# A mixed-precision 3x3 convolution on one core: image planes stored as a block of even rows and a block of odd rows

## The reference

```python
mask = _predictor_mask(x)                      # mean of 8x8 blocks >= 0.05
x_high = jnp.where(mask, x, EPS)
x_low = jnp.where(mask, EPS, x)
y_high = _conv(_quant_act_uint(x_high, act_scale_high, 8), _quant_weight_per_oc(w_high, 8))
y_low = _conv(_quant_act_uint(x_low, act_scale_low, 4), _quant_weight_per_oc(w_low, 4))
return y_high + y_low
```

## Time and profile before

| what | value |
|---|---|
| median of 3 runs | 664.49 us |
| the profiled execution's own time | 662.33 us |
| its span, first to last instruction | 660.5 us |
| busy share PE / DVE / ACT | 96% / 90% / 73% |
| mean granted TensorE clock | 0.996 |
| DMA, mean over the span | 158 GB/s |

### The profile page before, as it was taken

One profiled execution on the slowest core, in us unless ns is written; L12 is line 12 of the kernel. 1 busy time (PEld: TensorE's weight loads), 2 busy tenths in 40 slices (PEclk: granted clock), 3 DMA queues, 4 the chain that ended last, 5 costly groups with the idle time before them and its releaser, 6 DMA issues.

```text
span 660.5 us, 10672 instructions
## 1 busy us (share of the span) xinstructions
PE 635.5 (96%) x3714; PEld 355.9 (54%) x3714; DVE 594.5 (90%) x739; ACT 483.7 (73%) x491; POOL 10.2 (2%) x30
## 2 busy tenths in 40 slices
PE   3779999999999999999999999999999999999996
PEld 1345555555555555555555555555555555555554
DVE  7899999999999999999999999999999999999933
ACT  6768787777777778778777778777877877877442
POOL 3200000000000000000000000000000000000000
PEclk9989999999999999999999999999999999999999
DMA  6245445533435543334543344553343454331122
GB/s 266 97 154 195 162 174 195 194 134 128 182 140 194 194 158 124 163 146 188 194 186 127 132 177 157 194 194 148 122 175 139 194 194 170 124 150 68 72 97 98
DMA packets 14409, 104.07 MB, mean 158 GB/s; under 512 B 1728, under 2 KB 1728, under 8 KB 10432
## 3 DMA queue, kind: packets, MB, share of 16 engines
q1 hardware_dynamic: 14400, 103.95, 41.2%
HBM read 52.56 MB, written 51.38 MB: 157 GB/s over the span
## 4 chain that ended last, share of the span: by engine, by line
PE 95%; ACT 2%; DVE 1%; DMA 1%; issue 0%; DVEq 0%; SPq 0%
PE psum L336 95%; DMA wraw_l<-w_low 1%; ACT rounded_h L450 0%; ACT psum L485 0%; ACT wT_l L467 0%; DVE pooled L619 0%; DVE w_max_l L578 0%; ACT wT_h L467 0%; PE psum L322 0%; DVE ybuf L717 0%; DVEq L63 0%; DVE wq_l L601 0%; DVE wint_l L585 0%; DVE upper L701 0%; DVE wq_l L590 0%
## 5 line engine op out<-in xcount | busy, mean ns | idle before, releaser
L485 ACT ACTIVATE psum<-psum,ratio 128x1344 f32<-128x1344 f32 (+2 forms) x159 | 174.4, 1097 | 131.0 <-PE psum L336 128.3
L336 PE MATMUL psum<-plane_l,wT_l 128*128 128x448 f16 (+1 forms) x1164 | 211.7, 330 | 0.0
L336 PE MATMUL psum<-plane_h,wT_h 128*128 128x448 f16 (+1 forms) x1164 | 209.5, 328 | 0.0
L336 PEld LDWEIGHTS psum<-plane_l,wT_l 128*128 128x128 f16 x1164 | 112.9, 97 | 83.1 <-issue 2.4
L336 PEld LDWEIGHTS psum<-plane_h,wT_h 128*128 128x128 f16 x1164 | 112.0, 96 | 81.3
L717 DVE SCALAR_TENSOR_TENSOR ybuf<-psum,out_scale_h,shared 128x448 f32<-128x448 f32 (+1 forms) x194 | 114.3, 605 | 27.5 <-PE psum L336 20.1
L619 DVE TENSOR_REDUCE pooled<-xbuf 128x49 f32<-128x3136 f32 (+2 forms) x33 | 109.4, 3315 | 0.0
L506 ACT ACTIVATE shared<-psum,bias,out_scale_h 128x448 f32<-128x448 f32 (+1 forms) x128 | 86.2, 674 | 26.4 <-PE psum L336 23.5
L450 ACT ACTIVATE rounded_l<-xbuf,inv_act_l 128x1568 int16<-128x1568 f32 (+1 forms) x64 | 101.7, 1591 | 4.8 <-DMA xbuf<-x 4.8
L450 ACT ACTIVATE rounded_h<-xbuf,inv_act_h 128x1568 int16<-128x1568 f32 (+1 forms) x64 | 101.9, 1594 | 0.0
L336 PE MATMUL psum<-rowsum_l,wT_l 128*128 128x448 f16 (+1 forms) x384 | 86.9, 335 | 2.3 <-ACT wT_l L467 2.3
(11 more groups left out here) (78 smaller groups left out, 340.4 us busy)
## 6 DMA issues: line engine op xcount, KB each, us to landing
xbuf<-x SPq DMA_DIRECT2D x31, 1568.0 KB, 6.5
y<-ybuf SPq DMA_DIRECT2D x32, 896.0 KB, 3.6
y<-ybuf SPq DMA_DIRECT2D x32, 672.0 KB, 3.9
xbuf<-x SPq DMA_DIRECT2D x1, 896.0 KB, 7.9
xbuf<-x SPq DMA_DIRECT2D x1, 672.0 KB, 5.3
wraw_l<-w_low SPq DMA_DIRECT2D x1, 576.0 KB, 4.1
wraw_h<-w_high SPq DMA_DIRECT2D x1, 576.0 KB, 6.2
act_scales<-scales SPq DMA_DIRECT2D x1, 1.0 KB, 1.8
```

The costliest lines, as they stand in the source:

```text
L336: last = nc.tensor.matmul(out, wT[k][:, mat, :], moving(k, p, band, row, dx), start=(k == "l" and j == 0), stop=(j == len(parts) - 1), ski ...
L485: return nc.scalar.activation(banks, banks, ACT.Identity, scale=ratio[:, 0:1])
```

## The change

A plane is kept as two blocks: the padded even rows (0, 2, 4, ...), one after the other with a step of 58 elements, and behind them, at `ODD`, the padded odd rows. Rows d0 and d2 of all pairs then lie in the even block and d1 and d3 in the odd block, each pair one row further. `moving` reads every operand with a row step of `PITCH`. `apply_mask` writes image rows into the two blocks with two instructions in place of one, so `s_plane` counts twice as fast and those who wait on it wait for twice the count. `row_sums` and `differences` work on flat stretches of the two blocks; a stretch of row sums ends with the two border elements that GpSimd wrote before ("closing"). `outer` becomes two separate stretches, `inner` takes the common row step. The borders change their shapes, not their number.

```diff
-    PLANE = (H + 2) * PITCH + 4
+    ODD = (H // 2 + 1) * PITCH + 4
+    PLANE = 2 * ODD
...
             if row == "d1-d2":
-                return rows(inner[k][band][p], 1 + dx, INNER_PITCH, count)
+                return rows(inner[k][band][p][:, :], 1 + dx, PITCH, count)
             if row in ("d0-d2", "d1-d3"):
-                return rows(outer[k][band][p], (row == "d1-d3") * PITCH + 1 + dx, 2 * PITCH, count)
+                return rows(outer[k][band][p][:, int(row == "d1-d3"), :], 1 + dx, PITCH, count)
             if row is None:
-                return rows(rowsum[k][p], t0 * PITCH + 1 + dx, PITCH, count)
-            return rows(plane[k][p], (2 * t0 + row) * PITCH + 1 + dx, 2 * PITCH, count)
+                return rows(rowsum[k][p][:, :], t0 * PITCH + 1 + dx, PITCH, count)
+            return rows(plane[k][p][:, :], row % 2 * ODD + (t0 + row // 2) * PITCH + 1 + dx, PITCH, count)
...
-                nc.vector.tensor_tensor(
-                    rows(plane[k][p], (a0 * POOL + 1) * PITCH + 2, PITCH, (a1 - a0) * POOL
-                         ).rearrange("p (a y) w -> p a y w", y=POOL),
-                    clipped[k][:, elements(q)].rearrange("p (a y w) -> p a y w", y=POOL, w=W),
-                    mask[k][p][:, a0:a1, :].unsqueeze(2).to_broadcast([P, a1 - a0, POOL, W]),
-                    ALU.mult).then_inc(s_plane[k], 1)
+                for y, at in ((0, ODD), (1, PITCH)):
+                    nc.vector.tensor_tensor(
+                        rows(plane[k][p][:, :], at + a0 * POOL // 2 * PITCH + 2, PITCH, (a1 - a0) * POOL // 2
+                             ).rearrange("p (a y) w -> p a y w", y=POOL // 2),
+                        clipped[k][:, elements(q)].rearrange("p (a y s w) -> p a y s w", y=POOL // 2, s=2, w=W
+                                                             )[:, :, :, y, :],
+                        mask[k][p][:, a0:a1, :].unsqueeze(2).to_broadcast([P, a1 - a0, POOL // 2, W]),
+                        ALU.mult).then_inc(s_plane[k], 1)
...
-                nc.vector.tensor_tensor(rowsum[k][p][:, t0 * PITCH:t1 * PITCH].rearrange("p (t w) -> p t w", w=PITCH),
-                                        source(1), source(2), ALU.add).then_inc(s_rowsum[k], 1)
+                nc.vector.tensor_tensor(rowsum[k][p][:, at:at + size], flat[:, ODD + at:ODD + at + size],
+                                        flat[:, PITCH + at:PITCH + at + size], ALU.add).then_inc(s_rowsum[k], 1)
...
+                both = flat.rearrange("p (s n) -> p s n", s=2)
+                nc.vector.tensor_tensor(outer[k][band][p][:, :, :], both[:, :, at:at + size],
+                                        both[:, :, at + PITCH:at + PITCH + size], ALU.subtract).then_inc(s_diff[k], 1)
+                nc.vector.tensor_tensor(inner[k][band][p][:, :], flat[:, ODD + at:ODD + at + size],
+                                        flat[:, PITCH + at:PITCH + at + size], ALU.subtract).then_inc(s_diff[k], 1)
```

More of the change, by code:

```diff
@@ L54, in conv_program @@
     FIRST_MATS = TAPS + 6
-    INNER_PITCH = PITCH + 2
     BORDERS = 8
@@ L80, in conv_program @@
         rowsum = {k: [sb(f"rowsum_{k}{p}", [P, SUMS], F16) for p in range(2)] for k in "hl"}
-        outer = {k: {b: [sb(f"outer_{k}{b}{p}", [P, 2 * BAND[b][1] * PITCH + 2], F16) for p in range(2)] for b in FAST} for k in "hl"}
-        inner = {k: {b: [sb(f"inner_{k}{b}{p}", [P, BAND[b][1] * INNER_PITCH], F16) for p in range(2)] for b in FAST}
+        outer = {k: {b: [sb(f"outer_{k}{b}{p}", [P, 2, BAND[b][1] * PITCH + 2], F16) for p in range(2)] for b in FAST} for k in "hl"}
+        inner = {k: {b: [sb(f"inner_{k}{b}{p}", [P, BAND[b][1] * PITCH + 2], F16) for p in range(2)] for b in FAST}
                  for k in "hl"}
@@ L157, in conv_program, with rows @@
         block = ctx.enter_context(nc.Block())
-        def rows(buf, at, stride, count):
-            flat = buf[:, :]
+        def rows(flat, at, stride, count):
             return bass.AP(flat.tensor, flat.offset + at, [list(flat.ap[0]), [stride, count], [1, W]])
@@ L286, in borders @@
                 for k in "lh":
[L287 to L290, removed]
-                        shape = list(part.shape)
[L292 to L298, removed]
+                    flat = plane[k][p][:, :]
+                    last = H // 2 * PITCH
+                    sides = bass.AP(flat.tensor, flat.offset + 2 * PITCH,
+                                    [list(flat.ap[0]), [ODD - PITCH, 2], [PITCH, H // 2 - 1], [1, 2]])
+                    for part in (flat[:, 0:PITCH + 2], sides, flat[:, last + PITCH:ODD + 2],
+                                 flat[:, ODD + last:PLANE]):
+                        shape = list(part.shape)
+                        src = zero[:, :]
+                        for _ in shape[2:]:
+                            src = src.unsqueeze(2)
+                        nc.gpsimd.tensor_scalar(part, src.to_broadcast(shape), neg_q_eps[k][:, 0:1], 1.0, ALU.add,
+                                                ALU.mult).then_inc(s_border[p], 1)
             link = setup_link(pool, "gpsimd")
@@ L457, in masks @@
                     if not early(n):
-                        act.wait_ge(s_plane[k], prepared(n - 2))
+                        act.wait_ge(s_plane[k], 2 * prepared(n - 2))
                     nc.scalar.activation(mask[k][p][:, a0:a1, :].rearrange("p a (b x) -> p (a b) x", x=POOL),
@@ L645, in apply_mask @@
                     dve.wait_ge(s_high, TILES * BANDS * (n - 1))
-                nc.vector.tensor_tensor(
-                    rows(plane[k][p], (a0 * POOL + 1) * PITCH + 2, PITCH, (a1 - a0) * POOL
-                         ).rearrange("p (a y) w -> p a y w", y=POOL),
-                    clipped[k][:, elements(q)].rearrange("p (a y w) -> p a y w", y=POOL, w=W),
-                    mask[k][p][:, a0:a1, :].unsqueeze(2).to_broadcast([P, a1 - a0, POOL, W]),
-                    ALU.mult).then_inc(s_plane[k], 1)
+                for y, at in ((0, ODD), (1, PITCH)):
[6 more added lines that the diff above has]
+                        ALU.mult).then_inc(s_plane[k], 1)
             def row_sums(k, n, p, q=None):
                 a0, a1 = (0, BY) if q is None else PART[q]
-                t0, t1 = a0 * POOL // 2, a1 * POOL // 2
+                at, size = a0 * POOL // 2 * PITCH, (a1 - a0) * POOL // 2 * PITCH + 2
                 if early(n):
                     dve.wait_ge(s_border[p], BORDERS)
-                dve.wait_ge(s_plane[k], prepared(n, 1 if q is None else q))
+                dve.wait_ge(s_plane[k], 2 * prepared(n, 1 if q is None else q))
                 flat = plane[k][p][:, :]
-                def source(r):
-                    return bass.AP(flat.tensor, flat.offset + (2 * t0 + r) * PITCH,
-                                   [list(flat.ap[0]), [2 * PITCH, t1 - t0], [1, PITCH]])
-                nc.vector.tensor_tensor(rowsum[k][p][:, t0 * PITCH:t1 * PITCH].rearrange("p (t w) -> p t w", w=PITCH),
-                                        source(1), source(2), ALU.add).then_inc(s_rowsum[k], 1)
+                nc.vector.tensor_tensor(rowsum[k][p][:, at:at + size], flat[:, ODD + at:ODD + at + size],
+                                        flat[:, PITCH + at:PITCH + at + size], ALU.add).then_inc(s_rowsum[k], 1)
             def differences(k, n, p, band):
@@ L671, in differences @@
                     dve.wait_ge(s_border[p], BORDERS)
-                dve.wait_ge(s_plane[k], prepared(n))
+                dve.wait_ge(s_plane[k], 2 * prepared(n))
                 flat = plane[k][p][:, :]
                 t0, count = BAND[band]
[L675 to L682, removed]
+                at, size = t0 * PITCH, count * PITCH + 2
+                both = flat.rearrange("p (s n) -> p s n", s=2)
[3 more added lines that the diff above has]
+                                        flat[:, PITCH + at:PITCH + at + size], ALU.subtract).then_inc(s_diff[k], 1)
             def y_rows(p, band, e):
                 t0, count = BAND[band]
-                return rows(ybuf[p], (2 * t0 + e) * W, 2 * W, count)
+                return rows(ybuf[p][:, :], (2 * t0 + e) * W, 2 * W, count)
             def tile(band, name):
```

## The result

The changed kernel takes 652.82 us, the median of 6 runs between 650.36 and 653.17, against 663.18 us for the kernel before (6 runs, 661.83 to 666.38): ratio 0.9833, 95% interval 0.9811 to 0.9856, some 11 us less. The prediction for the median was 649.8, with a range from 646 to 657. Its direction, its place (TensorE's reading) and its range hold; its gain of 14.7 us is 3.6 us more than the 11.1 that the ratio makes of 663.18.

What follows compares the result with a forecast made beforehand. PE was taken as the bound: 14.3 us saved over 31 images plus 0.4 in the start-up make 14.7, from a median of 664.49 to 649.8 us. The range, to hold 8 times in 10, was 646 to 657.

Steps and rivals of the forecast that it cites:

- PE is the bound: Images 1 to 31: PE runs matmuls without gaps, 19.57 us an image; DVE has 18.33 us of work.
- DVE's flat form: Row sums and differences on DVE: flattening gains nothing, since strided rows pay no price; sizes change +1, +1 and -7 ns.
- The row step sorts the prices: PE's moving operands: steps of 58 and 60 elements are cheap, 116 in plane and outer dear; 193 against 199 ns.
- rowsum's 0.578 for three: Price for three 448-column matmuls at step 58, replacing plane's 0.597; saves 0.46 us an image, 14.3 us over 31.
- the range of 0.33 to 0.55 an image: PE's saving per image in us, given the 10 ns last digit of the view; 647 to 654 us in all.
- The start-up's 0.4 us: Image 0: PE's cheaper matmuls in its chain pieces save 0.38, called 0.4 us; nothing counted for DVE, ACT or DMA.
- DVE's extra instruction: Mask product on DVE, two instructions per plane in place of one: 0.16 to 0.33 us an image, hidden under PE.
- No change: Rival: plane and outer are dear for a reason other than row step; 664.5 us, chance 0.07.
- contention with DVE on the buffers: One reason offered by the no-change rival: DVE working on plane and outer makes their matmuls dear.
- The other reason that this rival gave: No-change rival: where the rows of plane and outer begin, not their step, makes their matmuls dear.
- The slower rival: Mask product halves on strided rows at one element a cycle: 3.25 us more an image, 735 us; chance 0.06.
- Half: Rival: step and first address both count, new blocks cost between 0.578 and 0.597 for three; 657 us, chance 0.07.

Runs made afterwards that it cites:

- the sweep: Small kernel of its own, no convolution: 30 back-to-back matmuls of 448 columns per row step and first element; step 58 189.3 to 195.7 ns, step 116 189.0 to 202.0.
- the sixth and eighth experiments: Changed kernel with all three taps reading from the same even element (output wrong): 637.63 us; changed kernel with pixels stored one element earlier: 645.29 us.
- the second execution of the changed one: The changed kernel run once more, unaltered, beside the pixels-from-element-1 version on the same chip: 651.66 us, ratio to before 0.9834.
- the third experiment: Kernel before with the mask product in two instructions, even and odd rows of the same old plane: 662.31 us, ratio 0.9988.
- the first two experiments: Kernel before with only TensorE's row step made 58: ratio 0.9832; changed kernel with step 116 again from image 1 on: ratio 0.9998.

## Why the prediction was right or wrong

**PE is the bound, and DVE's flat form is worth nothing: right.** The second experiment shows it, with all of the change but the step and 0.9998 of the time before. Row sums and differences kept their durations.

**The row step sorts the prices: right for this kernel, too simple as a rule.** Step 58 alone gives 594.95 us, step 116 alone 606.40. But the sweep has step 116 at 189 ns from element 0: step and first element work together, and the kernel before had its outer taps and the middle taps of its even rows at elements where the wide step is dear (200 to 204 and 198 ns; the middle taps of the odd rows, which begin at a multiple of four elements, took 188). The groups of three in which the prediction read its rows hid this: "its four bands start at different offsets at one price" was true of the three taps together, and the bands' offsets are all even.

**The new price, rowsum's 0.578 for three: this step failed, by its size.** "I take rowsum's value" priced a matmul in a stream of its own by one that stands behind twelve dear ones. In its own stream it costs 0.5807 (sweep), 0.9 ns a matmul more; the fifth experiment, all matmuls from rowsum's old addresses, ends at 595.01 us like the changed kernel. The gain of an image is 0.363 us in place of 0.46: 31 x 0.10 = 3 of the 3.6 us that lack; the rest is less than the runs of one kernel differ among themselves. I had even bounded the price from below with that row and called nothing cheaper, and put the upper end at no gain; the range of 0.33 to 0.55 an image holds the measured 0.363 near its low end. Why a matmul behind dear ones starts 0.9 ns earlier is not shown; that it follows from the neighbours and not from the addresses is, by the fifth experiment. Nor was rowsum's the lowest price to be had: the sixth and eighth experiments go below it with even first elements.

**The start-up's 0.4 us: borne out for the half that can be read.** The start of the long piece can't show it: it lies between 47.33 and 52.02 us over these executions, at 48.22 and 50.30 for the changed kernel alone. The pieces of image 0 show it where the granted clock was 1.00 in the kernel before and in the second execution of the changed one: the 30 matmuls went from 6.11 to 5.98 us and the last 15 from 3.13 to 3.06, 0.13 and 0.07 where the prediction had 0.15 and 0.075. The 45 between them ran partly at a lower clock in both.

**DVE's extra instruction, 0.16 to 0.33 us an image: right, at the low end.** 0.16 by the third experiment, hidden as foreseen; after the start-up PE never waits for DVE. DVE's own wait came to 0.80 us an image where the prediction had about 0.5, since PE gained less.

**The rivals.** No change falls by the first two experiments; contention with DVE on the buffers falls also by the sweep, where DVE is idle and the prices are the same. The other reason that this rival gave, where the rows begin, is half of the truth: at step 116 that decides between 189 and 202 ns. The Trainium skill, "TensorE: Matmul & The Clock Gate", section "Back-to-back issue gap", gives 448/2.4 + 2.5 = 189.2 ns as the gap of an isolated matmul; the sweep's streams agree for step 58 from elements 0 and 2 (189.3) and disagree for element 1 (195.7) and for step 116 (up to 202.0), for which it has no term. For a stream the same section has less, 131 ns at 512 columns, and no stream of 448 here comes below 189. The slower rival, DVE at half its rate on strided rows, falls by its 968 ns. Half's first clause, that step and first address both count, is right by the sweep; its second, that the new blocks begin at dearer addresses than rowsum's, falls: rowsum's own addresses cost as much (595.01), and moving the odd block by two elements changes nothing (594.94).

## What to carry to other kernels

Where PE is the bound, look at matmuls of equal shape that differ in start-to-start time: the row step and the first element of the moving operand are free to choose, and here they are worth 1.7% and another 1.0%. Put the more frequent taps on even elements, and try the row step rather than go by its size: of the eight in the sweep 56 to 60 were the cheapest and 116, not 128, the dearest. Take a price for a new stream from a stream of that kind, not from a cheap matmul between dear ones; a sweep of 175 us settles it.

## What the hardware showed that was not expected

A matmul whose rows begin at an odd 2-byte element costs 6.4 ns more for 8 rows at step 58, and next to nothing at step 56 (190 ns against 189). DVE pays nothing for writing its result to odd elements: a product of two 16-bit operands of 1568 elements stored from odd elements takes 971 ns, from even ones 969. The Trainium skill, "VectorE: DVE Perf Modes", section "What auto-detection actually checks", asks of the two-a-cycle mode 16 bits and a step of one; the trace agrees in so far as this product has both and keeps its time (no run here has another step). The Trainium skill's walk-through of that mode, in section "Mode 2×_1P — pack two bf16 into one 32-bit read", adds an alignment of 4 bytes, and there the trace disagrees for the output (971 ns); both inputs stayed on even elements.
